# Layer norm broadcasts over all 128 rows of the array instead of 32, in a four-layer transformer kernel

## What is computed

```python
def _layernorm(x, axis=-1, eps=1e-05):
    m = jnp.mean(x, axis=axis, keepdims=True)
    v = jnp.var(x, axis=axis, keepdims=True)
    return (x - m) / jnp.sqrt(v + eps)

h = jnp.concatenate([_L0_tok_ref(x, ...), txt], axis=1)
h = h + _L0_attn_ref(_layernorm(h, axis=-1), ...)   # gated attention
h = h + _L0_ffn_ref(_layernorm(h, axis=-1), ...)    # 32 experts, chosen by the experts
h = h + _L1_attn_ref(_layernorm(h, axis=-1), ...)   # spiking attention
h = h + _L1_ffn_ref(_layernorm(h, axis=-1), ...)    # 8 experts, top 2, and a shared one
```

## Time and profile before

| | us |
|---|---|
| median of three runs | 1883.24 (1882.54 to 1883.45) |
| the profiled execution | 1887.21 |
| its span, first to last instruction | 1885.6 |
| TensorE busy | 1449.3 (77%) |
| VectorE busy | 1158.9 (61%) |
| GpSimd busy | 811.6 (43%) |
| ScalarE busy | 691.1 (37%) |

### The profile page before, as it was taken

One profiled execution on the slowest core, in us unless ns is written; L12 is line 12 of the kernel. 1 busy time (PEld: TensorE's weight loads), 2 busy tenths in 40 slices (PEclk: granted clock), 3 DMA queues, 4 the chain that ended last, 5 costly groups with the idle time before them and its releaser, 6 DMA issues. The chain is left out here.

```text
span 1885.6 us, 28092 instructions
## 1 busy us (share of the span) xinstructions
PE 1449.3 (77%) x9073; PEld 1009.3 (54%) x9073; DVE 1158.9 (61%) x1778; ACT 691.1 (37%) x1151; POOL 811.6 (43%) x845
## 2 busy tenths in 40 slices
PE   5879999999854403877744863888898889999998
PEld 3457777777523302655532541333333468888887
DVE  2555555555367782111102488888887699989998
ACT  3124444444434301322210443887786611111110
POOL 1344444444310014788875103777771433333331
PEclk8569999999965656988875887999999899999999
DMA  4060000000001201444436000000000000000000
GB/s 157 1 259 3 0 0 0 0 0 0 1 7 18 78 18 46 86 80 77 80 49 191 5 0 2 2 1 0 0 1 29 10 5 13 13 13 13 13 13 17
DMA packets 69549, 61.11 MB, mean 32 GB/s; under 512 B 15629, under 2 KB 63515, under 8 KB 68203
## 3 DMA queue, kind: packets, MB, share of 16 engines
q1 hardware_dynamic: 52014, 47.52, 7.9%
q0 software_dynamic: 15744, 11.85, 4.5%
q10 hardware_dynamic: 1728, 0.94, 0.2%
HBM read 35.14 MB, written 25.18 MB: 32 GB/s over the span
## 5 line engine op out<-in xcount | busy, mean ns | idle before, releaser
L1772 PE MATMUL at_slot<-at_qm,at_ks 128*128 128x512 bf16 (+1 forms) x640 | 160.3, 384 | 19.2 <-DVE at_clip L1977 10.0
L1471 DVE TENSOR_SCALAR ex_y<-ex_ps_y,ex_rows 128x128 f32<-128x128 f32 (+1 forms) x96 | 29.2, 346 | 216.2 <-PE ex_ps_y L1418 118.2
L495 PE MATMUL ga_kv<-ga_kern,ga_v 128*128 128x274 f32 x512 | 133.5, 403 | 13.5 <-ACT ga_kern L584 12.6
L1375 POOL DMA_INDIRECT moe_sums<-ex_y,slot_sums x80 | 124.9, 1561 | 34.4 <-issue 20.7
L2493 DVE TENSOR_REDUCE mx_routed<-mx_weighted 128x128 f32<-128x1024 f32 x69 | 138.1, 2001 | 2.4
L2451 POOL TENSOR_TENSOR mx_h_E<-mx_hid_E,mx_h_E 128x768 fp32r<-128x768 f32 x23 | 43.6, 1896 | 189.1 <-DVE mx_h_E L2483 189.1
L1417 PE MATMUL ex_ps_y<-ex_down,ex_hid 128*128 128x128 f32 (+3 forms) x576 | 103.6, 333 | 24.8 <-ACT ex_hid L1458 20.8
L82 PE MATMUL mx_e<-ff_expert_out_high,mx_h_E 128*128 128x512 f32 x276 | 111.6, 404 | 12.2 <-DVE mx_weighted L2490 12.2
L1856 ACT ACTIVATE at_clip<-at_slot,at_four 128x1024 bf16<-128x1024 f32 (+1 forms) x96 | 106.8, 1112 | 31.9 <-PE at_slot L1772 30.1
L1977 DVE TENSOR_SCALAR at_clip<-at_slot 128x1024 bf16<-128x1024 f32 (+1 forms) x96 | 116.2, 1218 | 3.2 <-PE at_slot L1772 2.9
L495 PEld LDWEIGHTS ga_kv<-ga_kern,ga_v 128*128 128x128 f32 x512 | 92.2, 189 | 37.8 <-ACT ga_kern L584 16.8
(11 more groups left out here) (424 smaller groups left out, 3867.7 us busy)
## 6 DMA issues: line engine op xcount, KB each, us to landing
moe_sums<-ga_zeros SPq DMA_DIRECT2D x8, 1152.0 KB, 17.3
ar_rows<-moe_sums SPq DMA_DIRECT2D x32, 256.0 KB
ex_down<-in_down SPq DMA_DIRECT2D x32, 192.0 KB
token_rows<-ct_rows SPq DMA_DIRECT2D x17, 256.0 KB, 2.4
out_h<-H SPq DMA_DIRECT2D x22, 192.0 KB, 1.9
H<-in_text SPq DMA_DIRECT2D x1, 4096.0 KB, 21.0
patches<-in_patches SPq DMA_DIRECT2D x1, 1728.0 KB, 7.9
ga_sin<-in_sin SPq DMA_DIRECT2D x1, 1644.0 KB
```

The costliest lines, as they stand in the source:

```text
L495: last = nc.tensor.matmul(kv[:, e, 0:HALF], v[p][:, mt + 2 * side, e * P:(e + 1) * P], kern[(p + g) % 2][:, side, :], start=mt == 0 and si ...
L1375: nc.gpsimd.indirect_dma_start(out=sums, out_offset=bass.IndirectOffsetOnAxis(ap=scatter_idx[:, t, q:q + 1], axis=0), in_=y[q % 2][:, t, : ...
L1772: last = nc.tensor.matmul(to[r0:r0 + r, g % 2, :].rearrange("p (s n) -> p s n", s=2), ks[m][:, t * P:t * P + r], qm[m][:, 2 * g:2 * g + 2, ...
```

## The change

`pick_row_r` (32 rows used at a time) gives way to `pick_wide`, a table of four one-hot blocks with one block per group. In block `g` all rows but those of group `g` are zero. Every broadcast product now takes all 128 partitions of the table and of the `rstd` part. The number of products, their columns, their order and their waits stay as they are. Building the table takes four multiplications by zero and four copies of 32 rows on VectorE in `load_inputs`, where there was one cast. The table is 3 KB a partition larger; `W1` and `W2` move to memory that is given back after the gated attention.

```diff
@@ layernorm, and alike in router_norm and in the fourth norm
-                        last = nc.tensor.matmul(bc_ps[m % 2][:, j, 0:HALF], k["pick_row_r"][32 * g:32 * g + 32, j, :],
-                                                rstd_parts[i % 2][v][part][32 * g:32 * g + 32, :], start=part == 0, stop=part == 1)
+                        last = nc.tensor.matmul(bc_ps[m % 2][:, j, 0:HALF], k["pick_wide"][:, g, j, :],
+                                                rstd_parts[i % 2][v][part][:], start=part == 0, stop=part == 1)
@@ load_inputs
             dve.wait_ge(const_in, 16 * len(consts))
-            nc.vector.tensor_copy(k["pick_row_r"][:], k["pick_row"][:])
+            for g in range(NGRP):
+                nc.vector.tensor_scalar(k["pick_wide"][:, g], k["pick_row"][:], 0.0, None, ALU.mult).then_inc(cut, 1)
+            dve.wait_ge(cut, 6 + NGRP)
+            for g in range(NGRP):
+                nc.vector.tensor_copy(k["pick_wide"][32 * g:32 * g + 32, g], k["pick_row"][32 * g:32 * g + 32])
@@ build
-             "pick_row_r": sb("pick_row_r", [P, 2, P], F32R),
+             "pick_wide": sb("pick_wide", [P, NGRP, 2, P], F32R),
...
-        load_inputs(nc, x, k, H)
         with ExitStack() as st:
+            k["W1"] = st.enter_context(nc.sbuf_tensor("W1_sb", [P, 5 * P], F32))
+            k["W2"] = st.enter_context(nc.sbuf_tensor("W2_sb", [P, 2, P], F32))
+            load_inputs(nc, x, k, H)
```

More of the change, by code:

```diff
@@ L857, in broadcast @@
                     for half in range(2):
-                        last = nc.tensor.matmul(bc_ps[m % 2][:, j, 0:HALF], k["pick_row_r"][32 * g:32 * g + 32, j, :],
-                                                rstd_parts[i % 2][half][32 * g:32 * g + 32, :], start=half == 0, stop=half == 1)
+                        last = nc.tensor.matmul(bc_ps[m % 2][:, j, 0:HALF], k["pick_wide"][:, g, j, :],
+                                                rstd_parts[i % 2][half][:], start=half == 0, stop=half == 1)
                 last.then_inc(bc_done, 1)
@@ L2152, in broadcast @@
                     for part in range(2):
-                        last = nc.tensor.matmul(bc_ps[m % 2][:, j, 0:HALF], k["pick_row_r"][32 * g:32 * g + 32, j, :],
-                                                rstd_parts[i % 2][part][32 * g:32 * g + 32, :], start=part == 0, stop=part == 1)
+                        last = nc.tensor.matmul(bc_ps[m % 2][:, j, 0:HALF], k["pick_wide"][:, g, j, :],
+                                                rstd_parts[i % 2][part][:], start=part == 0, stop=part == 1)
                 last.then_inc(bc_done, 1)
@@ L2586, in build @@
         k = {"center": sb("center_sb", [P, P]), "mean_rows": sb("mean_rows_sb", [P, 2, 32]), "pick_row": sb("pick_row_sb", [P, 2, P]),
-             "pick_row_r": sb("pick_row_r", [P, 2, P], F32R),
-             "cols": sb("cols_sb", [P, NCOLS]), "ident": sb("ident_sb", [P, P]), "W1": sb("W1_sb", [P, 5 * P]),
-             "W2": sb("W2_sb", [P, 2, P]), "ones_bf": sb("ones_bf", [P, P], BF16), "b1_v3": sb("b1_v3", [P, EXPAND], BF16),
+             "pick_wide": sb("pick_wide", [P, NGRP, 2, P], F32R),
+             "cols": sb("cols_sb", [P, NCOLS]), "ident": sb("ident_sb", [P, P]), "ones_bf": sb("ones_bf", [P, P], BF16), "b1_v3": sb("b1_v3", [P, EXPAND], BF16),
              "down_b3": sb("down_b3", [P, NE * P], BF16),
```

## The result

The changed kernel takes 1863.49 us (median of four runs, 1862.82 to 1866.37), the kernel before in the same runs 1883.34. The gain by the medians is 19.85 us. The ratio on record is 0.9898, 95% interval 0.9881 to 0.9916. The forecast was 1859.8 with a gain of 23.4.

What follows compares the result with a forecast made beforehand. TensorE was taken as the bound, at half clock in the first norm. 12.2 + 2.5 + 4.8 + 1.3 + 2.6 = 23.4 us off 1883.2 gave 1859.8 us; range for 8 in 10: 1852 to 1874.

Steps and rivals of the forecast that it cites:

- The bound: First norm: TensorE, busy 36.74 of 37.40 us at clock 0.50, bounds it; in the others at the full clock.
- The clock and the rows: Broadcasts over 32 rows keep TensorE busy without lifting its clock; over 128 rows they should lift it, after about 4.1 us.
- Rival (a): The clock stays low in the first norm and only the switches go: gain 12.7 us, 1870.5; chance 0.13.
- The switches: Between centring and broadcast, each change of 128 and 32 rows loses 0.20 us, 0.30 at half clock; zero after.
- Rival (b): The clock rises but switches stay, belonging to fp32 against fp32r: 4.0 us a turn, 13.1 in all, 1870.1; chance 0.09.
- Rival (d): Slower: each 128-row weight load waits for the product before it, costing 18.6 us, 1901.8; chance 0.04.
- Rival (c): No change within 0.2%: VectorE's chain takes up what TensorE gives, 1881 to 1883; chance 0.06.
- First norm, two turns: From TensorE's rest to the variance, 7.2 us for 13.3, a gain of 6.1 a turn, 12.2 in two.
- First norm, end: Broadcasts without centrings, no switches: only the clock counts, 5.1 periods gain 0.5 each, 2.5 us.
- Second and third norm, turns: Two turns each at full clock: eight switches, 1.6 us, less 0.4 for a new wait; 1.2 x 4 = 4.8 us.
- Fourth norm, turns: ScalarE is nearly full and waits just 0.7 us for centrings in one turn: 2 x 0.65 = 1.3 us.
- Ends of the other norms: Ends of norms two to four, 7 to 16 us at half clock, gain some from a clock rise: 2.6 us.

## Why the prediction was right, and where its sum was off

**The bound.** Right. In the first norm TensorE at half the clock was the bound, and with the clock and the switches the norm became 15.4 us shorter, 14.8 of them behind its first inversion.

**The clock and the rows.** Right for this kernel, and incomplete as a rule. It rests on the end of the norm, where only the rows differ (0.50 throughout with 32, a rise after 5.8 us with 128), and on the turns with all switches kept, where it still rises. Rival (a), only the switches go, gave 12.7 us and falls with that. But the clock rose with 64 rows too, once, after 16.7 us, and with 32 rows and half the switches after 10.4 and 10.1 us in one kernel and not in 21.6 in another; and 128 rows with a switch around every broadcast raised nothing in an end. So the rows and the switches both decide how soon the clock rises. The prediction's sentence that products over 32 rows don't lift it is too strong. Which mixture of rows, gaps and switches the clock needs is open; no experiment varied them one by one.

**The switches.** Right. They were put at 0.20 us at the full clock and 0.30 at half. The pair went from 1.36 to 0.97 (0.39 for two) and from 2.42 to 1.83 (0.59 for two), and four added switches cost 0.78. Rival (b) falls as well, since the turns gain 7.0 and 5.7 and not 4.0. Rival (d), loads that wait, would have made the pair longer and falls by the same rows. Rival (c), VectorE takes up the gain, falls with the measured time, though in the three shorter norms it was partly true (below).

**First norm, two turns.** Forecast 12.2, measured 12.7 (7.0 and 5.7), and between 10.7 and 12.6 in the other traces with the same turns, by how late the clock rises. So the agreement to half a microsecond is partly luck; the range of 5.3 to 6.5 a turn is what the prediction earned. From the rest to the variance the forecast was 7.2 us; it is 7.13 in the first turn, and 7.69 in the second, where the clock rose after 4.5 instead of 3.4 us. The first turn gained 0.9 more than its stretch, mainly because the variance, 16 products, now runs at the full clock (1.46 us, has 2.08), and the inversion behind it starts that much sooner. One premise was wrong and did no harm: the rest of some 4 us that "stays" in each turn stood only in the first. In the second turn of the kernel before, TensorE at half the clock was still working and rested 0.65 us (70.83 to 71.48); now it rests 4.69 in both.

**First norm, end.** Forecast 2.5, measured 2.1. VectorE's timeline, against the earlier trace rows:

```profile
81.77 0.72 DVE L238 TENSOR_TENSOR ln_for_h<-HN,ln_bcast 128x548 f32<-128x548 f32 x1 [0.74 <-PE ln_bcast L152]
...
90.93 1.36 DVE L238 TENSOR_TENSOR HN<-HN,ln_bcast 128x548 f32<-128x548 f32 x2 [0.29 <-PE ln_bcast L152]
92.52 1.37 DVE L238 TENSOR_TENSOR HN<-HN,ln_bcast 128x548 f32<-128x548 f32 x2 [0.23 <-PE ln_bcast L152]
```

A period at the full clock is 1.59 us (90.93 to 92.52), forecast 1.6. The clock rose later than assumed, after 5.8 us instead of 4.1.

**Second and third norm, turns.** Forecast 2.4 for each norm, measured 1.9 and 1.7 from inversion to inversion. The term was mis-sized at the new wait. The third broadcast of a turn stands behind the first scaling, and that behind the inversion: of the third norm's steps above, two take 1.44 and 1.34 us (the latter from 1035.21 to 1036.55) and the one with the wait 1.87 (1033.34 to 1035.21), no less than the 1.83 of before. I had given this wait 0.4 of the 1.6; it takes 0.8.

**Fourth norm, turns.** Forecast 1.3, measured nothing: from inversion to inversion 8.79 us after (1458.26 to 1467.05) and 8.78 before. What failed is the reading of the earlier trace rows. I took 0.7 us of ScalarE's idle time before the centrings for what a faster TensorE could fill. The idle time has moved instead: ScalarE waits 1.7 us in a turn before and after, 0.7 for centrings and 0.5 for scalings before, 0.5 and 0.7 after, and 0.5 for the variance in both. ScalarE's timeline after:

```profile
1460.07 0.40 ACT L2210 ACTIVATE ff_tokens<-ln_centred 128x274 f32<-128x274 f32 x1 [0.53 <-PE ln_centred L2133]
...
1462.02 0.84 ACT L2201 ACTIVATE ff_tokens<-ff_tokens,cols_sb 128x548 f32<-128x548 f32 x1 [0.68 <-DVE ff_tokens L2274]
```

and TensorE's:

```profile
1463.20 1.19 PE L2133 MATMUL ln_centred<-H,center_sb 128*128 128x274 f32 x4 [0.39 <-ACT ff_tokens L2210]
```

At 1462.02 ScalarE waits 0.68 us for the first scaling of VectorE, which stands behind the inversion; the copies of the centred tokens stand behind that on ScalarE, and TensorE waits for a bank from them. I read a turn as a ring from inversion through scaling, ScalarE, centring and variance back to inversion, with TensorE's switches beside it. The waits fit this, but no run cut the ring.

**Ends of the other norms.** Forecast 1.0, 0.6 and 1.0, measured 0.3, 0.5 and 0.95. The one of the second norm failed. TensorE's timeline there:

```profile
517.68 1.28 PE L862 MATMUL ln_bcast<-ln_rstd,pick_wide 128*128 128x274 f32 x4 [3.83 <-DVE XN L997]
...
526.26 1.01 PE L862 MATMUL ln_bcast<-ln_rstd,pick_wide 128*128 128x274 f32 x4 [2.32 <-DVE XN L997]
```

The distance is 8.58 us, and before it was also 8.58 (534.75 to 543.33). Between its broadcasts VectorE also works on the softmax of the router, TensorE rests 3.83 and 2.32 us for it, and the clock is low from 516.4 us on but for 3.4, as it was before from 534.5.

**The sum.** By norm, forecast against two executions, both counted from the first inversion: 14.7 against 14.8 and 14.6; 3.4 against 2.2 and 2.2; 3.0 against 2.2 and 2.2; 2.3 against 0.9 and 0.9. The first norm, where TensorE had no rival, came out as worked. All of the 3.5 us that are missing lie in the three norms where another engine's chain ran close beside it. The load stage costs nothing that shows, as forecast: the first norm's first centring stands at 27.0 us before and at 27.2 and 27.1 after.

**What the profile was to show.** The clock between 0.5 and 1, the 7 to 8 us, the end of the norm (forecast 95, it is 93.9) and the unchanged gated attention all came. The start distances of 0.50 and 0.91 did not appear as such, since the trace puts a broadcast 0.26 us behind its centring and the next centring 0.71 behind that; their sum, the pair, is what holds. In the third norm two centrings and a broadcast take 1.44 and 1.34 us where nothing is waited for (forecast 1.42 to 1.6), and 1.87 where VectorE is.

## What to carry to other kernels

Where TensorE is busy without a gap and its granted clock is still low, look at how many rows its products use and at how often the number changes: short products between full ones cost a switch on either side, and the price can be read as start distance less the columns' time. Before you pad such products to 128 rows, try to put two of them in different row groups next to each other, which alone made the first norm 11.2 us shorter where the change made it 15.4, most of that at half the clock. And count a saving on TensorE in full only where its waits name no other engine; where two chains run close, draw the ring first.

## What the runs showed of the hardware that I had not expected

- 64 rows cost the same at a switch as 32 (1.21 us a step at half the clock, 0.66 at the full one), and did little for the clock: with 64-row broadcasts and 128-row centrings TensorE was busy 16.30 of 16.30 us at 0.50 before it rose.
- With 32 rows and half the switches the clock rose after 10.4 and 10.1 us of work without a gap, with 128 rows after 3.2 to 6.9 us.
- Broadcasts over 128 rows with a four-column product over 32 rows ahead of each stayed at 0.50 for 24 us, busy 21.21 of them. In the turns, where centrings stand between, the same broadcasts let it rise after 6.9 and 4.6 us.
- Two broadcasts in different groups of 32 rows took 1.22 us at half the clock, one takes 1.21.
- A cast of 274 columns took 0.30 us alone, 0.90 beside GpSimd's squaring and 1.30 beside its additions, so an order of VectorE that looks better can be worth nothing.
